# Attention and feed-forward layer on one core: x loaded once, split in rows, and turned by transposing transfers

## The chip, the cores and the metric

The kernel runs on 1 core of one Trainium2 chip. The metric is the device time of one execution, in microseconds (us); before the change it is 1840.24, the median of 3 runs (1839.78 to 1840.81). Engines are named as in the profile: PE is TensorE (matmuls, with PEld its weight loads), DVE VectorE, ACT ScalarE, POOL GpSimd, SP the engine whose queue issues the transfers.

## The reference

x has 8 sequences of 1024 tokens and 512 features. A layer of segmented attention with a memory is followed by a layer norm, then a feed-forward with quantized weights and a second layer norm:

```python
xs = x.reshape(b, n_seq, 128, d)                  # segments of 128 tokens
q, k, v = proj(Wq), proj(Wk), proj(Wv)            # 8 heads of 64
# for each segment, in order, with mem and z carried along:
sq = elu(q) + 1; att_mem = sq @ mem / (sq @ z)
sk = elu(k) + 1; mem = mem + sk^T v; z = z + sum(sk)
att = gate * att_mem + (1 - gate) * softmax(q k^T / 8) @ v
x = layernorm(x + att @ Wo)
h = relu(x @ quantize(W1)^T + b1)                 # 2048 wide
x = layernorm(x + h @ quantize(W2)^T + b2)
```

## The kernel before

The work is cut into 32 groups g, each of two sequences (t = 0, 1) at one segment of 128 tokens; two groups are alive at a time (LIVE = 2), so the memory of group g comes from group g - 2. Weights stay in SBUF. Operands of matmuls are float16 pairs: a high part and the rest, so that a product takes three matmuls (high by high, high by low, low by high). Each engine has its own hand-written order of work; in the loop `for g in range(2, NG + 2)` all engines work on the projections, scores and softmax of group g beside the feed-forward of g - 2 and g - 1. Semaphores alone tie the orders together.

PE in one turn of the loop (lines 577 to 616): `ffn_up(g-2, 1..4)`, `project_qk(g)` with `ffn_up(g-2, 5..7)` between, `project_out(g-1)`, `update_memory(g-1)`, `scores(g)`, `ffn_down(g-2, 0)`, `project_v(g)`, `ffn_down(g-2, 1, 0)`, `read_memory(g)` (line 378), the rest of `ffn_down`, `attend(g)` (lines 392 to 394), `ffn_up(g-1, 0)`. `read_memory(g, 0)` takes two PSUM banks that held scores of t = 1, so it waits for `p_lo(g, 1, 1)` (line 761). `ffn_up(g-1, 0)` waits for `attm`, the last piece of `read_scale(g, 1)` on DVE.

x before the change comes twice. `load_x` (line 1559) brings the rows of a group, needed for the residual, in one transfer. `load_blocks` (line 1572) brings the same values in 8 transfers of 64 KB, arranged so that DVE's 32 x 32 transpose (`turn_x`, line 696) completes the turning. Then:

- `group_max` (line 631) on DVE: largest |x| per partition, over `x_blocks`.
- `bounce_out` (line 1613) and `bounce_back` (line 1620) on SP: 128 values to DRAM and back, so that each partition has all of them.
- `all_max` (line 644) and `x_scale`, four small DVE instructions in a chain (the last is line 661).
- `xt_hi` (line 1170) on ACT and `xt_lo` (line 702) on DVE: the scaled, split, turned x in `xt`, 718 and 1096 ns each on average.
- `project_qk` and `project_v` on PE read `xt`.

Only group 0 has its x turned by PE. Three transposing transfers on SP are there already: `turn_p` (the softmax, line 1647), `turn_y` (line 1656) and `turn_att` (line 1639); the last two are of the size that x has, 128 x 1024 values of float16 to a t. `move_sk` (line 1632) issues 16 small transfers.

Ahead of the loop stands a start-up part in which PE also transposes the feed-forward weights (`turn_w`, line 280), ACT puts them (`put_w`, line 1296), and DVE rounds them (`round_w`, line 930). `turn_w(n)` waits for `put_w(n-2)`, so the two go in step. `sum_all(2)` on PE waits for a sum (line 919) that DVE forms behind `qk_split(1, "k", 0)`. `attend(0, 1)` waits for `turn_p(0, 1)`. `spread_bias_max` (line 514) waits for `bias_maximum` (line 940), which DVE does behind `att_scale(0, 1)`.

Of the kernel before, what the change touches and what calls it, by code (L numbers as in the profile page):

```python
# [32 lines left out]
    xblocks skblocks xturn xt_hi xt kproj qproj kq_exp klo qlo elu vproj v_hi v1 v  # L33
# [7 lines left out]
def build_program(nc, x, Wq, Wk, Wv, betas, Wo, W1, b1, W2, b2, out):  # L41
# [14 lines left out]
    with ctx:  # L56
# [31 lines left out]
        x_blocks = sb("x_blocks", [P, TG, D])  # L88
# [90 lines left out]
        def in_cols(blocks, t):  # L179
            return blocks[:, t].rearrange("p (k c) -> p k c", k=KT)  # L180

# [21 lines left out]
        def by_middle(g, t):  # L203
            return TG * (g - 1) + t + 1

# [38 lines left out]
        def _(pe):  # L244
# [38 lines left out]
            def project_qk(g, n, j):  # L283
# [6 lines left out]
                pe.wait_ge(sem["xt"], by_t(g, 1))  # L290
# [9 lines left out]
            def project_v(g, t):  # L300
# [5 lines left out]
                pe.wait_ge(sem["xt"], by_t(g, t))  # L306
# [312 lines left out]
        def _(dve):  # L619
            def group_max(g):  # L620
                if not 0 <= g < NG:
                    return
                if g == 0:
                    dve.wait_ge(s_x[0], 16)
                else:
                    dve.wait_ge(sem["xblocks"], 16 * 8 * g)
# [4 lines left out]
                dve.tensor_reduce(amax[:, g % 2:g % 2 + 1], x_blocks[:] if g else rows[:, 0], AX_XY, ALU.max,  # L631
# [60 lines left out]
            def turn_x(g, t):  # L692
                if not 0 <= g < NG:
                    return
                dve.wait_ge(sem["xblocks"], 16 * 8 * g)
                dve.transpose(x_blocks[:, t], x_blocks[:, t]).then_inc(sem["xturn"], 1)

            def xt_lo(g, t):
# [3 lines left out]
                dve.scalar_tensor_tensor(out=xt[:, t, KT:2 * KT], in0=in_cols(x_blocks, t) if g else x_bank(t), scalar=gcol(g, G_SCALE), in1=xt[:, t, 0:KT],  # L702
# [366 lines left out]
            turn_x(2, 0)  # L1069
            turn_x(2, 1)  # L1070
# [25 lines left out]
            for g in range(2, NG + 2):  # L1096
# [11 lines left out]
                h_split(g - 2, 7)  # L1108
                score_max(g, 0, 0)
# [4 lines left out]
                group_max(g + 1)  # L1114
# [6 lines left out]
                turn_x(g + 1, 0)  # L1121
                turn_x(g + 1, 1)
# [11 lines left out]
                all_max(g + 1)  # L1134
                x_scale(g + 1, 0)
# [3 lines left out]
                x_scale(g + 1, 1)  # L1139
                x_scale(g + 1, 2)  # L1140
                x_scale(g + 1, 3)
# [18 lines left out]
        def _(act):  # L1160
            def xt_hi(g, t):
                if not 0 <= g < NG:
                    return
                act.wait_ge(sem["xscale"], 4 * g + 4)
                if g:
                    act.wait_ge(sem["vproj"], by_t(g - 1, t))
                    act.wait_ge(sem["kproj"], 2 * g)
                    act.wait_ge(sem["qproj"], 2 * g)
                act.wait_ge(sem["xturn"], by_t(g, t))
                act.activation(xt[:, t, 0:KT], in_cols(x_blocks, t) if g else x_bank(t), ACT.Copy, scale=gcol(g, G_SCALE)).then_inc(sem["xt_hi"], 1)  # L1170
# [202 lines left out]
            for g in range(2, NG + 2):  # L1373
# [27 lines left out]
                v_split(g, 1)  # L1401
# [339 lines left out]
```

## Time and profile before

| | before |
|---|---|
| median of 3 runs | 1840.24 us |
| the profiled execution, its own time | 1839.69 us |
| its span, first to last instruction | 1837.9 us |
| PE busy | 1783.5 us (97%) |
| DVE busy | 1461.5 us (80%) |
| ACT busy | 997.0 us (54%) |
| POOL busy | 781.8 us (43%) |
| mean busy share of the DMA queue q1 | 45.6% of 16 engines |
| granted TensorE clock, mean | 0.99 |
| chain that ended last, share of PE | 95% |

A time in the trace is counted from the start of the span; 1.8 us of the execution lie around it. A busy engine is not necessarily what sets the end: the chain of work that ended last and the waits of an engine tell that. PE has 54.4 us in which it does nothing.

### The profile page before, as it was taken

Reading aid. Unit: us, or ns where it says so; the run is one execution under the profiler, and the core shown is the slowest. Engines: PE = TensorE matmul, PEld = TensorE weight load, DVE = VectorE, ACT = ScalarE, POOL = GpSimd, SP = SyncE. Lnnn points to the kernel's source line nnn. Section 1 sums busy time; section 2 is a strip of 40 time slices with the busy share of each in tenths; the row PEclk is TensorE's granted clock in tenths of the full one; section 3 lists DMA queues with packets and bytes.
Section 4 is the critical chain, followed back from the end, with each engine's and each line's share of the span. In section 5 each row is a group of like instructions: output and inputs, shape, how many; then the busy total and the mean of one; then the engine's idle time right before and its main releaser. Section 6 shows DMA issues by size and latency. Waiting matters only on the chain.

```text
span 1837.9 us, 42414 instructions
## 1 busy us (share of the span) xinstructions
PE 1783.5 (97%) x15935; PEld 1249.6 (68%) x15935; DVE 1461.5 (80%) x2807; ACT 997.0 (54%) x2422; POOL 781.8 (43%) x775
## 2 busy tenths in 40 slices
PE   4779999999999999999999999999999999999998
PEld 3556777766777766677766677766677776677765
DVE  7667788878888887888887888887878887888774
ACT  5765645555655555554655554655564555565542
POOL 0203444543444444354444354444344453444442
PEclk9889999999999999999999999999999999999999
DMA  8624435455445455435445534445543544443320
GB/s 281 150 38 78 74 73 90 59 88 87 73 76 93 61 84 91 83 67 90 71 72 93 86 66 85 77 66 94 87 71 78 86 63 89 89 74 73 60 47 24
DMA packets 555130, 150.87 MB, mean 82 GB/s; under 512 B 528544, under 2 KB 532528, under 8 KB 554416
## 3 DMA queue, kind: packets, MB, share of 16 engines
q1 hardware_dynamic: 554928, 148.16, 45.6%
q8 instruction: 129, 2.11, 0.5%
q14 instruction: 73, 0.60, 0.2%
HBM read 50.54 MB, written 16.80 MB: 37 GB/s over the span
## 4 chain that ended last, share of the span: by engine, by line
PE 95%; DVE 2%; ACT 2%; issue 1%; POOL 0%; DMA 0%; POOLq 0%; ACTq 0%; DVEq 0%
PE bank L464 12%; PE bank L465 12%; PE bank L448 12%; PE bank L449 12%; PE bank L294 6%; PE bank L295 6%; PE bank L296 6%; PE bank L378 3%; PE bank L426 3%; PE bank L428 3%; PE bank L427 3%; PE bank L308 3%; PE bank L310 3%; PE bank L309 3%; PE bank L413 2%; PE bank L327 1%
## 5 line engine op out<-in xcount | busy, mean ns | idle before, releaser
L448 PE MATMUL bank<-yt,w1t 128*128 128x256 f16 x2048 | 454.0, 273 | 0.6 <-ACT arena L1271 0.4
L449 PE MATMUL bank<-yt,w1t 128*128 128x256 f16 x2048 | 453.9, 273 | 0.0
L464 PE MATMUL bank<-w2t,arena 128*128 128x512 f16 x1024 | 388.7, 380 | 0.0
L465 PE MATMUL bank<-w2t,arena 128*128 128x512 f16 x1024 | 388.1, 379 | 0.0
L1271 ACT ACTIVATE arena<-bank,b_scaled,wscalars 128x256 f32<-128x256 f32 x512 | 261.2, 564 | 179.9 <-PE bank L449 108.6
L1215 ACT ACTIVATE bank<-bank,exp_bias,gscalars 128x128 f32<-128x128 f32 x512 | 220.5, 431 | 222.1 <-DVE exp_bias L752 222.1
L448 PEld LDWEIGHTS bank<-yt,w1t 128*128 128x128 f16 x2048 | 200.4, 98 | 24.2 <-ACT arena L1271 0.7
L449 PEld LDWEIGHTS bank<-yt,w1t 128*128 128x128 f16 x2048 | 200.4, 98 | 22.8
L875 DVE CAST arena<-arena 128x512 f16<-128x512 f32 x256 | 186.0, 727 | 7.5 <-ACT arena L1271 7.4
L1508 POOL TENSOR_TENSOR arena<-arena 128x512 f16<-128x512 f32 x128 | 155.2, 1213 | 68.6 <-DVE arena L875 68.6
L464 PEld LDWEIGHTS bank<-w2t,arena 128*128 128x128 f16 x1024 | 100.1, 98 | 118.6
L1430 POOL TENSOR_TENSOR att_mem<-att_mem,gate_in 128x512 f32<-128x512 f32 x60 | 76.1, 1268 | 239.2 <-DVE att_mem L791 239.2
L465 PEld LDWEIGHTS bank<-w2t,arena 128*128 128x128 f16 x1024 | 100.3, 98 | 113.4
L1170 ACT ACTIVATE xt<-x_blocks,gscalars 128x512 f16<-128x512 f32 x62 | 44.5, 718 | 220.7 <-DVE gscalars L661 220.6
L1452 POOL TENSOR_SCALAR var_eps<-mean_var 128x1 f32<-128x1 f32 x64 | 14.7, 229 | 326.5 <-DVE mean_var L856 326.5
L702 DVE SCALAR_TENSOR_TENSOR xt<-x_blocks,gscalars,xt 128x512 f16<-128x512 f32 x62 | 67.9, 1096 | 93.0 <-ACT xt L1170 93.0
L295 PE MATMUL bank<-xt,wk_hi 128*128 128x256 f16 x512 | 141.3, 276 | 0.0
L294 PE MATMUL bank<-xt,wk_hi 128*128 128x256 f16 x512 | 141.3, 276 | 0.0
L296 PE MATMUL bank<-xt,wk_lo 128*128 128x256 f16 x512 | 141.2, 276 | 0.0
L1473 POOL TENSOR_TENSOR y_rows<-rows,y_rows 128x512 f16<-128x512 f32 x60 | 68.1, 1156 | 171.6 <-ACT y_rows L1253 171.6
L294 PE MATMUL bank<-xt,wq_hi 128*128 128x256 f16 x512 | 139.5, 273 | 0.0
L296 PE MATMUL bank<-xt,wq_lo 128*128 128x256 f16 x512 | 139.5, 273 | 0.0
(180 smaller groups left out, 4358.5 us busy)
## 6 DMA issues: line engine op xcount, KB each, us to landing
rows<-in_L_attn_x SPq DMA_DIRECT2D x32, 512.0 KB, 3.9
out_rows<-rows SPq DMA_DIRECT2D x64, 256.0 KB, 2.4
x_blocks<-in_L_attn_x SPq DMA_DIRECT2D x248, 64.0 KB, 3.0
sk<-sk_t SPq DMA_DIRECT2D x480, 32.0 KB, 2.0
arena<-in_L_ffn_W SPq DMA_DIRECT2D x6, 1024.0 KB, 5.6
w2t<-in_L_ffn_W SPq DMA_DIRECT2D x2, 1024.0 KB, 13.1
w1t<-in_L_ffn_W SPq DMA_DIRECT2D x2, 1024.0 KB, 14.2
amax_row<-amax_dram SPq DMA_DIRECT2D x31, 64.0 KB, 3.1
```

The source lines that it names most:

```text
L294: pe.matmul(ps[:, :, c], w_hi[n][:, k, cols], xt[:, :, k], start=k == 0, stop=False)
L295: pe.matmul(ps[:, :, c], w_hi[n][:, k, cols], xt[:, :, KT + k], start=False, stop=False)
L296: ins = pe.matmul(ps[:, :, c], w_lo[n][:, k, cols], xt[:, :, k], start=False, stop=k == KT - 1)
L448: pe.matmul(ps[:, c], w1t[:, k, cols], yt[:, g % 2, :, k], start=k == 0, stop=False)
L449: ins = pe.matmul(ps[:, c], w1t[:, k, cols], yt[:, g % 2, :, KT + k], start=False, stop=k == KT - 1)
L464: pe.matmul(banks[own][:], h_hi[:, f, toks], w2t[:, f, :], start=f == 0, stop=False)
L465: ins = pe.matmul(banks[own][:], h_lo[:, f, toks], w2t[:, f, :], start=False, stop=f == FT - 1)
L875: dve.tensor_copy(hi, h32[:, n % NH32]).then_inc(sem["h_hi"], 1)
L1215: ins = act.activation(ps[:, c], ps[:, c], ACT.Exp, scale=gcol(g, G_EXP), bias=exp_bias[:, t, at:at + 1], accum_out=row_sum[:, t, h:h + 1])
L1271: ins = act.activation(h32[:, n % NH32, c * GT:(c + 1) * GT], ps[:, c], ACT.Relu, scale=w(H_SCALE_Y), bias=b1_scaled[:, f:f + 1])
L1430: pool.tensor_tensor(a, a, gate_in[:], ALU.mult).then_inc(sem["gated_in"], 1)
L1508: pool.tensor_tensor(lo, h32[:, n % NH32], hi, ALU.subtract).then_inc(sem["h_pool"], 1)
```

## The change

For all groups but 0, x comes once, in rows. ACT and DVE scale and split it in rows (into a new buffer `x_rows`, in the place of `x_blocks`), and two transposing transfers on SP put both halves into `xt`. The 8 block transfers and DVE's two transposes of a group go. The maximum is taken over the rows, and stands earlier in DVE's order: directly behind `h_split(g-2, 7)`, ahead of `score_max(g, 0, 0)`. `all_max`, `x_scale`, `xt_hi` and `xt_lo` stand earlier too, in front of or between `v_split(g, 1)`, `read_scale` and `residual(g-2, 0, 1)`. In the start-up, `xt_hi(1)` stands ahead of `put_w(0)`, and `project_qk(1, "k", 0)` behind `turn_w(11)` instead of ahead of `turn_w(8)`.

```diff
@@ buffers
-        x_blocks = sb("x_blocks", [P, TG, D])
+        x_rows = sb("x_rows", [P, TG, 2, D], F16)
+        def xt_there(g, t):
+            return (sem["xt"], t + 1) if g == 0 else (sem[f"xt{t}"], 16 * g)
@@ PE: project_qk and project_v
-                pe.wait_ge(sem["xt"], by_t(g, 1))
+                pe.wait_ge(*xt_there(g, 0))
+                pe.wait_ge(*xt_there(g, 1))
@@ PE, start-up
-            project_qk(1, "k", 0)
             for n in range(8, 12):
                 turn_w(n)
+            project_qk(1, "k", 0)
             sum_all(2)
@@ DVE: group_max
-                if g == 0:
-                    dve.wait_ge(s_x[0], 16)
-                else:
-                    dve.wait_ge(sem["xblocks"], 16 * 8 * g)
+                dve.wait_ge(s_x[g % NX], 16 * (g // NX + 1))
...
-                dve.tensor_reduce(amax[:, g % 2:g % 2 + 1], x_blocks[:] if g else rows[:, 0], AX_XY, ALU.max,
+                dve.tensor_reduce(amax[:, g % 2:g % 2 + 1], rows[:, g % NX], AX_XY, ALU.max,
@@ DVE: turn_x goes; xt_lo
+                if g:
+                    dve.scalar_tensor_tensor(out=x_rows[:, t, 1], in0=rows[:, g % NX, t], scalar=gcol(g, G_SCALE), in1=x_rows[:, t, 0],
+                                             op0=ALU.mult, op1=ALU.subtract).then_inc(sem["xt_lo"], 1)
+                    return
@@ DVE, start-up
             x_scale(1, 0)
-            turn_x(1, 0)
             x_scale(1, 1)
-            turn_x(1, 1)
             x_scale(1, 2)
             x_scale(1, 3)
             round_w(1)
+            xt_lo(1, 0)
+            xt_lo(1, 1)
             scale_sums(0, 0)
             scale_sums(0, 1)
             bias_columns()
-            xt_lo(1, 0)
             att_scale(0, 0)
-            xt_lo(1, 1)
@@ DVE, loop
                 h_split(g - 2, 7)
+                group_max(g + 1)
                 score_max(g, 0, 0)
...
                 p_lo(g, 0, 0)
-                group_max(g + 1)
                 score_max(g, 1, 0)
...
                 p_lo(g, 1, 0)
-                turn_x(g + 1, 0)
-                turn_x(g + 1, 1)
                 p_lo(g, 1, 1)
                 v_split(g, 0)
                 turn_sk(g)
                 invert_sums(g, 0)
+                all_max(g + 1)
+                x_scale(g + 1, 0)
                 v_split(g, 1)
+                x_scale(g + 1, 1)
+                x_scale(g + 1, 2)
                 read_scale(g, 0)
+                x_scale(g + 1, 3)
                 read_scale(g, 1)
+                xt_lo(g + 1, 0)
+                xt_lo(g + 1, 1)
                 residual(g - 2, 0, 1)
...
-                all_max(g + 1)
-                x_scale(g + 1, 0)
...
-                xt_lo(g + 1, 0)
                 att_scale(g, 1)
-                xt_lo(g + 1, 1)
@@ ACT: xt_hi
+                    if g > 1:
+                        act.wait_ge(sem[f"xt{t}"], 16 * (g - 1))
+                    act.wait_ge(s_x[g % NX], 16 * (g // NX + 1))
+                    ins = act.activation(x_rows[:, t, 0], rows[:, g % NX, t], ACT.Copy, scale=gcol(g, G_SCALE))
@@ ACT, start-up
             w_sum(2, 0)
-            for n in range(0, 4):
+            xt_hi(1, 0)
+            xt_hi(1, 1)
+            for n in range(0, 8):
                 put_w(n)
-            xt_hi(1, 0)
-            for n in range(4, 8):
-                put_w(n)
-            xt_hi(1, 1)
             w_sum(2, 1)
-            qk_split(1, "k", 0)
             for n in range(8, 12):
                 put_w(n)
+            qk_split(1, "k", 0)
@@ ACT, loop: xt_hi(g+1, 0) and (g+1, 1) stand directly behind v_split(g, 1)
@@ SP: load_blocks goes; new
+            def turn_x(g, t):
+                if not 0 <= g < NG:
+                    return
+                sp.wait_ge(sem["xt_lo"], TG * (g - 1) + t + 1)
+                sp.wait_ge(sem["kproj"], 2 * g)
+                sp.wait_ge(sem["qproj"], 2 * g)
+                sp.wait_ge(sem["vproj"], by_t(g - 1, t))
+                sp.dma_start_transpose(xt[:, t], x_rows[:, t].rearrange("p c n -> p (c n)")).then_inc(sem[f"xt{t}"], 16)
@@ SP, start-up (in the place of load_blocks(1) stands load_x(1); turn_x(1, 0..1) ahead of move_sk(0), turn_x(2, 0..1) ahead of move_sk(1))
@@ SP, loop
             for g in range(2, NG + 2):
-                load_blocks(g + 1)
                 bounce_out(g + 1)
                 turn_p(g, 0)
                 turn_y(g - 1, 0)
                 turn_y(g - 1, 1)
+                bounce_back(g + 1)
                 turn_p(g, 1)
-                bounce_back(g + 1)
+                turn_x(g + 1, 0)
+                turn_x(g + 1, 1)
                 move_sk(g)
```

## Rows read from the trace of the kernel before

**Rows 1.** Busy time by stretch: one period; us, PE, PEld, DVE, ACT, POOL, PEclk, DMA.

```profile
957.80:1012.50 54.70, 54.70 (x499) 38.31 (x497) 45.22 (x87) 29.85 (x74) 24.31 (x24) 1.00 0.49 80
```

**Rows 2.** Waits of PE from 130 us on, the longest in total.

```profile
PE bank L392 <- issue: 0.6, 1, 0.6
```

**Rows 3.** Timeline of ACT in the start-up: start, length, instruction, idle before.

```profile
60.08 1.29 ACT L1296 ACTIVATE w1t<-bank,unround 128x512 f16<-128x512 f32 x2
...
63.44 0.71 ACT L1170 ACTIVATE xt<-x_blocks,gscalars 128x512 f16<-128x512 f32 x1
```

**Rows 4.** Timeline of DVE in the start-up.

```profile
61.09 0.70 DVE L696 STREAM_TRANSPOSE x_blocks<-x_blocks 128x512 f32<-128x512 f32 x1
...
62.51 0.16 DVE L661 RECIPROCAL gscalars<-gscalars 128x1 f32<-128x1 f32 x1
...
79.14 0.15 DVE L919 TENSOR_REDUCE wscalars<-wscalars 128x1 f32<-128x4 f32 x1
```

**Rows 5.** Timeline of PE in the start-up.

```profile
67.92 0.19 PE L392 MATMUL bank<-v_hi,pt 128*128 128x64 f16 x1 [0.69 <-issue]
...
71.28 0.38 PE L514 MATMUL bank<-wscalars,ones_all 1*128 1x1 f32 x2 [2.50 <-DVE wscalars L940]
...
75.89 1.04 PE L280 MATMUL bank<-ident,arena 128*128 128x128 f32 x8
78.53 1.24 PE L280 MATMUL bank<-ident,arena 128*128 128x128 f32 x8 [1.61 <-ACT w1t L1296]
```

**Rows 6.** Busy time by stretch (columns as in rows 1), behind PE's 2.50 us of idleness.

```profile
72.10:75.50 3.40, 3.40 (x18) 2.34 (x17) 3.09 (x15) 0.00 (x0) 0.29 (x1) 0.50 0.31 48
```

**Rows 7.** Timeline of SP's queue in the start-up: turn_p(0, 1).

```profile
58.30 5.99 SPq L1647 DMA_TRANSPOSE pt<-p_rows  x1
```

**Rows 8.** Timeline of DVE, POOL and PEld within one period.

```profile
926.21 0.68 DVE L747 TENSOR_REDUCE row_max<-bank 128x4 f32<-128x512 f32 x1
926.95 1.15 POOL L1508 TENSOR_TENSOR arena<-arena 128x512 f16<-128x512 f32 x1
927.03 1.10 DVE L752 TENSOR_SCALAR exp_bias<-row_max,gscalars 128x4 f32<-128x4 f32 x1
...
928.86 0.23 DVE L752 TENSOR_SCALAR exp_bias<-row_max,gscalars 128x4 f32<-128x4 f32 x1
...
931.42 1.21 DVE L631 TENSOR_REDUCE amax<-x_blocks 128x1 f32<-128x1024 f32 x1
...
939.19 0.69 DVE L761 SCALAR_TENSOR_TENSOR p_rows<-bank,p_rows 128x512 f16<-128x512 f32 x1 [0.54 <-ACT p_rows L1226]
...
940.52 0.64 PEld L378 LDWEIGHTS bank<-mem,sq_t 64*128 64x128 f32 x10 [0.42 <-issue]
```

**Rows 9.** Timeline of SP's queue within the same period.

```profile
919.12 0.39 SPq L1559 DMA_DIRECT2D rows<-in_L_attn_x  x1
...
942.56 3.00 SPq L1647 DMA_TRANSPOSE pt<-p_rows  x1
...
946.28 11.23 SPq L1632 DMA_DIRECT2D sk<-sk_t  x16
```

**Rows 10.** Timeline of DVE and PE, rest of the period and the next one's start.

```profile
909.55 1.18 DVE L722 SCALAR_TENSOR_TENSOR sk_t<-exp_tmp,relu_tmp 128x512 f32<-128x512 f32 x1
...
942.02 0.16 DVE L768 RECIPROCAL inv_sum<-row_sum 128x8 f32<-128x8 f32 x1
...
949.04 0.27 PE L448 MATMUL bank<-yt,w1t 128*128 128x256 f16 x1
...
957.78 0.27 PE L294 MATMUL bank<-xt,wk_hi 128*128 128x256 f16 x1
```

**Rows 11.** The page, issues: KB each, median us from issue to landing.

```profile
rows<-in_L_attn_x SPq DMA_DIRECT2D x32, 512.0 KB, 3.9
...
amax_row<-amax_dram SPq DMA_DIRECT2D x31, 64.0 KB, 3.1
...
at<-att_dot SPq DMA_TRANSPOSE x60, 3.1
```

More of the change, by code:

```diff
@@ L32 @@
     amax amax_row amax_cell amax_all xscale sc0 sc1 sc2 sc3
-    xblocks skblocks xturn xt_hi xt kproj qproj kq_exp klo qlo elu vproj v_hi v1 v
+    skblocks xturn xt_hi xt_lo xt xt0 xt1 kproj qproj kq_exp klo qlo elu vproj v_hi v1 v
     score rowmax exp_bias pexp pt_hi pt_lo pt0 pt1 skturn
@@ L690, in scalars @@
                     dve.tensor_scalar(gcol(g, G_WO), gcol(g, G_AINV), w(INV_W["o"]), None, ALU.mult).then_inc(sem["sc3"], 1)
[L692 to L696, printed above, removed]
             def xt_lo(g, t):
@@ L701, in xt_lo @@
                 dve.wait_ge(sem["xt_hi"], by_t(g, t))
[L702 removed]
+                if g:
+                    dve.scalar_tensor_tensor(out=x_rows[:, t, 1], in0=rows[:, g % NX, t], scalar=gcol(g, G_SCALE), in1=x_rows[:, t, 0],
+                                             op0=ALU.mult, op1=ALU.subtract).then_inc(sem["xt_lo"], 1)
+                    return
+                dve.scalar_tensor_tensor(out=xt[:, t, KT:2 * KT], in0=x_bank(t), scalar=gcol(g, G_SCALE), in1=xt[:, t, 0:KT],
                                          op0=ALU.mult, op1=ALU.subtract).then_inc(sem["xt"], 1)
@@ L1165, in xt_hi @@
                 if g:
[L1166 to L1170, printed above, removed]
+                    if g > 1:
+                        act.wait_ge(sem[f"xt{t}"], 16 * (g - 1))
+                    act.wait_ge(s_x[g % NX], 16 * (g // NX + 1))
+                    ins = act.activation(x_rows[:, t, 0], rows[:, g % NX, t], ACT.Copy, scale=gcol(g, G_SCALE))
+                else:
+                    act.wait_ge(sem["xturn"], t + 1)
+                    ins = act.activation(xt[:, t, 0:KT], x_bank(t), ACT.Copy, scale=gcol(g, G_SCALE))
+                ins.then_inc(sem["xt_hi"], 1)
             def qk_split(g, n, j):
@@ L1401, in _ @@
                 v_split(g, 1)
+                xt_hi(g + 1, 0)
+                xt_hi(g + 1, 1)
                 if g - 1 in EDGES:
@@ L1405, in _ @@
                     yt_hi(g - 1, 1)
-                xt_hi(g + 1, 0)
                 h_relu(g - 1, 0)
                 h_relu(g - 1, 1)
-                xt_hi(g + 1, 1)
                 h_relu(g - 1, 2)
@@ L1559, in load_x @@
                 sp.dma_start(rows[:, g % NX], src).then_inc(s_x[g % NX], 16)
-            def load_blocks(g):
+            def turn_x(g, t):
                 if not 0 <= g < NG:
                     return
-                b0, seg, _ = place(g)
-                if g > 1:
-                    sp.wait_ge(sem["xt"], by_t(g - 1, 1))
-                for t in range(TG):
-                    src = x[b0 + t, seg * P:(seg + 1) * P, :].rearrange("(b j) (k a i) -> a j k b i", j=32, a=4, i=32)
-                    for a in range(4):
-                        dst = x_blocks[32 * a:32 * a + 32, t].rearrange("p (k b i) -> p k b i", k=KT, b=4)
-                        sp.dma_start(dst, src[a]).then_inc(sem["xblocks"], 16)
+                sp.wait_ge(sem["xt_lo"], TG * (g - 1) + t + 1)
[3 more added lines that the diff above has]
+                sp.dma_start_transpose(xt[:, t], x_rows[:, t].rearrange("p c n -> p (c n)")).then_inc(sem[f"xt{t}"], 16)
             def load_w(n):
@@ L1677, in _ @@
             sp.dma_start(b2_all[:], b2.partition_broadcast(P)).then_inc(sem["b2_load"], 16)
-            load_blocks(1)
+            load_x(1)
             load_ffn_w(2, 0)
@@ L1686, in _ @@
             turn_p(0, 1)
+            turn_x(1, 0)
+            turn_x(1, 1)
             move_sk(0)
-            load_x(1)
             load_x(2)
             load_ffn_w(2, 2)
-            load_blocks(2)
             load_ffn_w(2, 3)
+            load_x(3)
             bounce_out(2)
@@ L1696, in _ @@
             bounce_back(2)
+            turn_x(2, 0)
+            turn_x(2, 1)
             move_sk(1)
@@ L1699, in _ @@
             turn_att(1, 1)
-            load_x(3)
             for g in range(2, NG + 2):
-                load_blocks(g + 1)
                 bounce_out(g + 1)
```

9 lines of the change are left out of this document (1 added, 8 removed).

## The prediction

> **What bounds the kernel now.** I read the windows first, one for each turn of the loop. A turn lasts 54.70 us and PE is busy in all of it, at the full clock [rows 1]. The waits of PE from 130 us on say the same: the longest is 0.6 us, once [rows 2]. So in the loop nothing that is taken off DVE, SP or the transfers can shorten the time: DVE is busy 45 of 54.7 us, yet PE never stands for it. A gain can come only from PE's 54 idle us, nearly all in the start-up, and a loss from a piece that now reaches PE late. Both need timelines, of the start-up and of one turn. There the reader is to look at the start of a PE instruction and at the end of what releases it.
>
> **The loop, part by part.** *Removed:* 8 block transfers, two DVE transposes of 0.70 us [rows 4]. Worth nothing: PE covers them. If that cover went, each transpose would be worth its 0.70.
>
> *The maximum, moved ahead of score_max(g, 0, 0).* It reads rows that load_x issues at 919.12 and that land 3.9 us later, 923.0 [rows 9, 11]; DVE comes to it at 926.21 [rows 8]. So it does not wait, with 3.2 us to spare. Its 1.21 us now stand in front of the scores' maximum. But exp_bias is held behind a POOL subtraction until 928.1, and takes 1.10 us instead of 0.23 [rows 8]. With the maximum in front it would start at 926.21 + 1.13 + 0.82 = 928.16, when POOL is through, and end at 928.39 instead of 928.13. So ACT's exponentials, and p_lo at the end of their chain, come 0.3 us later. p_lo(g, 1, 1) ends at 939.88 and read_memory begins at 940.52: 0.6 us to spare [rows 8]. I take no wait; the bounds of the shift are 0 and 1.21.
>
> *The way round through DRAM.* Before, the values went out when the maximum ended, at 932.6 [rows 8]; now at 927.4. bounce_back takes the place of turn_p(g, 1), which was issued at 942.56 [rows 9], and lands 3.1 us later [rows 11]: 945.7 at the latest. DVE reaches all_max at about 942.4, behind invert_sums [rows 10] and the 0.3 us. Wait: 0 to 3.3 us. SP's queue was slow there with the small transfer to DRAM ahead of the transposes; that is now 5 us earlier, so I take 0. What stands behind: v_split(g, 1), x_scale, both read_scale, some 4 us, and then ffn_up(g-1, 0) may start; it starts at 949.04 [rows 10]. Without the wait DVE is there at 946.5, 2.5 us ahead.
>
> *Split and turn.* xt_hi follows at about 945.4 and takes 0.71 [rows 3] twice; xt_lo follows read_scale(g, 1), 1.1 us each, so it ends between 948 and 949. A transposing transfer of this size lands 3.1 us after its issue [rows 11], and the second is issued over a us behind the first: xt is there by 951 to 953. project_qk begins at 957.78 [rows 10]. About 5 us to spare.
>
> By the Trainium skill (SBUF — State Buffer, "Who interferes with whom") a DVE instruction with two inputs in SBUF is shut out for the whole of a POOL instruction that reads SBUF. That speaks against xt_lo here, beside POOL's gating: it would put some 1.5 us on each xt_lo; the 5 us still cover it, and the sum is the same by both.
>
> *What is moved behind it.* residual(g-2, 0, 1) comes about 3 us later, and with it POOL's second variance, add_bias and the gating. Their reader on ACT, at_hi(g, 1), stands behind h_relu of the next turn, over a us later: covered. move_sk (16 issues, 11.2 us from 946.28 [rows 9]) now waits for the two turns of x, until about 950 to 951, and ends, with its last landing, near 963; the next writing of sk_t, which waits for it, is at 909.55 + 54.7 = 964.2 [rows 1, 10]. Covered by about 1 us, and behind that DVE's own room before the next scores. turn_p(g, 1) has one short issue put in front, but a queue less crowded: the 0.6 us of attend(g, 1) [rows 2], which I ascribe to a late turned softmax, should go. **Loop: -0.6 us.**
>
> **The start-up**, where PE is the bound only in part.
> 1. xt_hi(1) now stands ahead of put_w(0). The scale is ready at 62.67 [rows 4], less some 0.9 for the two transposes between: 61.8. ACT then does two xt_hi of 0.71 [rows 3]. put_w(0) starts near 63.0 instead of 60.08 [rows 3]: +2.9. Until then ACT stands idle.
> 2. PE's turn_w(2) to (7) go in step with put_w: +2.9. attend(0, 1) waited 0.69 us before, for its turned softmax [rows 5]; this is absorbed: 70.1 instead of 67.92, +2.2.
> 3. Between attend(0, 1) and spread_bias_max lay 3.4 us, and PE idle for 2.50 of them [rows 5]. In it DVE waited for ACT's second xt_hi and did xt_lo(1, 1) and a rounding, which now come before. So the distance shrinks: I take +0.7 for spread_bias_max (bounds 0 and +2.2), which ends at 72.4.
> 4. turn_w(8) to (11) come next: 1.04 + 1.24 us [rows 5] and a short wait. project_qk(1, k, 0) starts at 74.9 instead of 71.66 [rows 5]: **+3.2**. The turned x is issued once turn_p(0, 1) is off SP, at 64.3 [rows 7], and so lands near 70: it does not set this.
> 5. project_qk(1, k, 0) took 4.2 us, to 75.89, 3.4 of them at the half clock, 1.2 GHz, behind PE's 2.50 idle us [rows 5, 6]. Now it comes behind transposes with about 1 us of idleness; I take the full clock: **-1.7** (bounds -1.7 and 0). It ends at 77.4.
> 6. sum_all(2) needs the sum at 79.14 [rows 4], which stands on DVE behind qk_split(1, k, 0): 3.4 us after the projection's end. Before, turn_w(8) to (11) filled that time, until 79.77 [rows 5]. Now nothing does, and PE idles 3.7 us. No term of its own (the sum now comes at 77.4 + 3.7 = 81.1, 1.5 later than before), but the clock: behind 2.50 idle us a stretch of 3.4 us ran at the half clock [rows 6], and this idleness is longer. Half of 3.40: **+1.7** (bounds 0 and 1.7).
> Behind it every step waits for the one before on PE, ACT or DVE until the loop, so nothing is given back. **Start-up: 3.2 - 1.7 + 1.7 = +3.2**, with bounds +1.5 and +4.9. The fewer transfers there are worth nothing: the weights' loads wait for splits on DVE.
>
> By the Trainium skill (TensorE: Matmul & The Clock Gate, "What's actually happening") idleness throttles PE and work releases it. It says nothing other than rows 6 about the second hole, but it makes the terms of steps 5 and 6 differ between executions, as the moment of the switch is not tied to the kernel.
>
> **The sum.** The profiled execution took 1839.69 us (span 1837.9 and 1.8 around it), 0.55 below the median. 1839.69 + 3.2 - 0.6 = 1842.3; as a median, 1842.9 (+0.14%).
>
> **The rivals.**
> *A: the way back from DRAM is late in every turn.* If bounce_back is issued only at 942.56, as turn_p was, and lands at 945.7, DVE stands 3.3 us in front of all_max, and the 4.1 us of work behind it end at 949.8, against 949.04 [rows 9 to 11]. PE stands 0.75 us in each of 30 turns: +22, 1865. It decides once the values land later than about 944.9. For it: that turn's queue. Against: the queue should be freer. Chance 0.12.
> *B: the maximum delays the softmax in full.* If p_lo(g, 1, 1) shifts by 1.21 instead of 0.3, it passes the margin of 0.64 by 0.57 [rows 8]: 30 x 0.57 = +17, 1860. It decides at a shift of 0.64. Against: the arithmetic on exp_bias. Chance 0.10.
> *C: the start-up gives the delay back*, say because PE's later holes absorb it: 1839.5 to 1840.5. Against: those holes follow the scores, which are themselves late. Chance 0.10.
> *D: faster.* No row has 3.7 us for it: only the 0.6, and a start-up in which the half clock is escaped and step 1 is nearly hidden, 1836. Chance 0.06.
> The forecast has 0.62.
>
> **Range and chances.** About 0.2%, 3.7 us, is what a measurement of this kernel can tell from no change: 1836.6 to 1843.9. The forecast's own bounds are +1.5 - 0.6 and +4.9 - 0.6, so 1841.1 to 1844.5; its upper end, above 1843.9, gets 0.12. Slower: 0.12 + 0.12 + 0.10 = 0.34. Same: 0.50 + 0.10 = 0.60. Faster: 0.06. The range runs from 1839 to 1860: it takes in C and most of B, and leaves out A's far end and D, under 2 in 10. The likeliest case's own is 1841.1 to 1844.5.
>
> **What would show it.** Right: turns of 54.7 us with PE busy throughout; project_qk(1, k, 0) near 75, then a hole of 3.7 us before sum_all(2); DVE busy some 40 us less (62 transposes at 0.70); the 0.6 us gone. Wrong: a wait of PE in every turn ahead of ffn_up (A) or read_memory (B), or of project_qk on a transfer; or a loop that starts no later than before (C).

## The result, and the profile after

The changed kernel takes 1846.97 us, the median of 6 runs (1845.01 to 1847.83), beside 1840.18 of the kernel before (1839.64 to 1840.81, 6 runs): a ratio of 1.0036, 95% interval 1.0026 to 1.0045. It is slower by 6.8 us. The profiled execution took 1846.83 us, with a span of 1845.0. One run of e12 (7124 us) and two of the kernel before in the batches of the experiments (3613 and 6618 us) fell into a slow state and are left out of all ranges and ratios below.

The page, busy time and the shares of the chain that ended last:

```profile
PE 1784.8 (97%) x15935; PEld 1250.0 (68%) x15935; DVE 1411.5 (77%) x2745; ACT 1003.4 (54%) x2422; POOL 763.7 (41%) x775
...
PE 68%; DVE 12%; ACT 6%; POOL 4%; issue 4%; SPq 3%; DMA 3%; ACTq 0%; DVEq 0%; POOLq 0%
```

DVE is busy 50 us less than before, and PE as long as before; yet the chain, 95% PE before, now goes through DVE, ACT, POOL, SP's queue and a transfer. PE's idle time has grown.

Busy time by stretch, for three turns of the loop in the changed kernel (columns as in [rows 1]):

```profile
467.70:522.40 54.70, 54.70 (x498) 38.31 (x497) 41.95 (x81) 30.16 (x74) 22.87 (x24) 1.00 0.45 79
522.40:577.60 55.20, 54.81 (x499) 38.41 (x498) 43.09 (x85) 30.05 (x74) 24.01 (x25) 1.00 0.46 79
...
907.50:963.80 56.30, 55.02 (x499) 38.47 (x498) 44.64 (x88) 29.94 (x74) 25.02 (x27) 1.00 0.43 78
```

The first is like the turn of [rows 1]: 54.70 us, PE busy in all of it. The other two are longer. Measured from the start of one project_qk(g, k, 0) to the next, the turns g = 9, 10 and 13 to 18 take 54.86 to 56.22 us, the rest 54.70. That makes +4.8 us. Before, one turn was longer by 0.8, which is gone: the loop stands at **+4.0**. Group 2's projection starts at 139.5 us instead of 136.5: the start-up stands at **+3.0**.

The waits of PE from 130 us on, against [rows 2]:

```profile
PE bank L379 <- DVE p_rows L757: 3.3, 7, 0.7
PE bank L328 <- DVE rows L841: 0.8, 2, 0.6
```

read_memory (L379) waits for p_lo (L757), the end of the softmax. And DVE's own waits from 130 us on:

```profile
DVE gscalars L642 <- DMA amax_row<-amax_dram: 27.5, 23, 2.0
...
DVE sk_t L718 <- DMA sk<-sk_t: 3.1, 3, 2.5
```

In 23 turns DVE stands in front of all_max (L642) because the maximum is not back from DRAM. Here is that place in a turn that stays at 54.70 (it starts at 303.6), SP's queue first, then DVE, with the next maximum (L629) and what comes before it:

```profile
340.00 0.53 SPq L1607 DMA_DIRECT2D amax_row<-amax_dram  x1
...
343.06 0.29 DVE L642 TENSOR_REDUCE gscalars<-amax_row 128x1 f32<-128x128 f32 x1
...
360.48 1.37 DVE L859 TENSOR_SCALAR rows<-rows,mean_var,rstd 128x512 f32<-128x512 f32 x1 [2.00 <-POOL rstd L1450]
...
376.94 0.75 DVE L841 SCALAR_TENSOR_TENSOR rows<-bank,gscalars,rows 128x512 f32<-128x512 f32 x1 [0.59 <-PE bank L429]
...
379.53 0.75 DVE L841 SCALAR_TENSOR_TENSOR rows<-bank,gscalars,rows 128x512 f32<-128x512 f32 x1 [0.89 <-PE bank L429]
...
381.49 1.22 DVE L629 TENSOR_REDUCE amax<-rows 128x1 f32<-128x1024 f32 x1
```

And in the turn that starts at 522.4, with what PE does at the end:

```profile
559.53 0.54 SPq L1607 DMA_DIRECT2D amax_row<-amax_dram  x1
...
564.41 0.29 DVE L642 TENSOR_REDUCE gscalars<-amax_row 128x1 f32<-128x128 f32 x1 [1.89 <-DMA amax_row<-amax_dram]
...
581.82 1.37 DVE L859 TENSOR_SCALAR rows<-rows,mean_var,rstd 128x512 f32<-128x512 f32 x1 [2.00 <-POOL rstd L1450]
...
597.61 0.75 DVE L841 SCALAR_TENSOR_TENSOR rows<-bank,gscalars,rows 128x512 f32<-128x512 f32 x1
...
599.24 0.75 DVE L841 SCALAR_TENSOR_TENSOR rows<-bank,gscalars,rows 128x512 f32<-128x512 f32 x1
...
601.54 1.21 DVE L629 TENSOR_REDUCE amax<-rows 128x1 f32<-128x1024 f32 x1
...
614.79 0.69 DVE L757 SCALAR_TENSOR_TENSOR p_rows<-bank,p_rows 128x512 f16<-128x512 f32 x1 [1.76 <-ACT p_rows L1219]
...
615.58 1.67 PE L379 MATMUL bank<-mem,sq_t 64*128 64x65 f32 x26 [0.49 <-DVE p_rows L757]
```

Read the square brackets. In both turns DVE waits 2.00 us for POOL's variance (L1450): that wait is no slack, since POOL got its input from DVE and moves with it. What is slack is the 0.59 and 0.89 us in which DVE waits for PE's project_out (L429): 1.48 us in all. In the late turn (522.4) all_max starts 2.55 us later within the turn (42.01 against 39.46), those two gaps are gone, and the next maximum starts 1.25 us later (79.14 against 77.89). Behind it come the scores, ACT's exponentials and p_lo, and PE stands. The way back decides once all_max starts behind about 39.5 + 1.5 = 41 us of a turn. In this kernel it starts anywhere from 39.4 to 42.9, and the trace divides cleanly: the eight turns that follow an all_max at 41.08 us or later are the eight late ones, and no turn that follows one at 40.84 or earlier is late.

The start-up, PE (against [rows 5]), SP's queue and DVE:

```profile
64.01 1.97 PE L280 MATMUL bank<-ident,w2t 128*128 128x128 f32 x8 [4.86 <-ACT w1t L1289]
...
72.31 0.38 PE L515 MATMUL bank<-wscalars,ones_all 1*128 1x1 f32 x2 [1.04 <-DVE wscalars L936]
...
81.20 0.38 PE L507 MATMUL bank<-wscalars,ones_all 128*128 128x1 f32 x2 [3.29 <-DVE wscalars L915]
...
66.88 10.56 SPq L1619 DMA_DIRECT2D sk<-sk_t  x16
...
80.40 0.68 DVE L718 SCALAR_TENSOR_TENSOR sk_t<-exp_tmp,relu_tmp 128x512 f32<-128x512 f32 x1
```

PE stands 4.86 us for put_w(0), 1.04 for the bias's maximum, and 3.29 in front of sum_all(2), the hole of the prediction's step 6. The last two rows come up again: move_sk(0), now issued from 66.88 us on, behind the turned x, and DVE's writing of the tile that it reads, without a wait here.

### The profile page after: what moved, and what is told of

Its sections match the earlier page's. It is cut to its first block, busy times and chain, and to the rows that moved or that the text cites. A ratio compares the mean times of both kernels' runs of the same rounds, so it can differ in the third digit from the quotient of the medians.

```text
span 1845.0 us, 42230 instructions
## 1 busy us (share of the span) xinstructions
PE 1784.8 (97%) x15935; PEld 1250.0 (68%) x15935; DVE 1411.5 (77%) x2745; ACT 1003.4 (54%) x2422; POOL 763.7 (41%) x775
## 4 chain that ended last, share of the span: by engine, by line
PE 68%; DVE 12%; ACT 6%; POOL 4%; issue 4%; SPq 3%; DMA 3%; ACTq 0%; DVEq 0%; POOLq 0%
PE bank L449 9%; PE bank L450 9%; PE bank L465 9%; PE bank L466 8%; PE bank L295 4%; PE bank L296 4%; PE bank L297 4%; ACT bank L1208 3%; PE bank L379 2%; PE bank L427 2%; PE bank L429 2%; PE bank L428 2%; DMA amax_row<-amax_dram 2%; PE bank L309 2%; PE bank L311 2%
## 5 line engine op out<-in xcount | busy, mean ns | idle before, releaser
L1421 POOL TENSOR_TENSOR att_mem<-att_mem,gate_in 128x512 f32<-128x512 f32 x60 | 81.5, 1359 | 291.3 <-DVE att_mem L787 291.3
L871 DVE CAST arena<-arena 128x512 f16<-128x512 f32 x256 | 193.0, 754 | 8.5 <-ACT arena L1264 8.4
L757 DVE SCALAR_TENSOR_TENSOR p_rows<-bank,p_rows 128x512 f16<-128x512 f32 x128 | 88.5, 692 | 140.5 <-ACT p_rows L1219 140.5
L1499 POOL TENSOR_TENSOR arena<-arena 128x512 f16<-128x512 f32 x128 | 148.6, 1161 | 74.7 <-DVE arena L871 74.7
L859 DVE TENSOR_SCALAR rows<-rows,mean_var,rstd 128x512 f32<-128x512 f32 x128 | 104.6, 838 | 60.3 <-POOL rstd L1450 60.3
L874 DVE TENSOR_TENSOR arena<-arena 128x512 f16<-128x512 f32 x128 | 145.4, 1136 | 4.4
L1180 ACT ACTIVATE exp_tmp<-bank,gscalars 128x512 f32<-128x512 f32 x128 | 87.8, 686 | 101.4 <-DVE sk_t L718 98.4
```

Source lines behind the costliest of these rows:

```text
L871: dve.tensor_copy(hi, h32[:, n % NH32]).then_inc(sem["h_hi"], 1)
L874: dve.tensor_tensor(lo, h32[:, n % NH32], hi, ALU.subtract).then_inc(sem["h_dve"], 1)
L1499: pool.tensor_tensor(lo, h32[:, n % NH32], hi, ALU.subtract).then_inc(sem["h_pool"], 1)
```

## The experiments

Three theories were open for the loop: the values come back late (the one I held by now), the maximum ahead of the scores uses up the softmax's margin (the prediction's rival B), the transfers of sk are late of themselves. For the start-up: my six steps, against rival C. All edits are to the changed kernel. In this table "late" counts turns over 54.75 us among g = 2 to 29, and "group 2" is when its projection starts; both are of the profiled execution, the rest of all runs.

| run | median (range), us | ratio to before, 95% | late | group 2 |
|---|---|---|---|---|
| changed | 1846.97 (1845.0 to 1847.8) | 1.0036 (1.0026 to 1.0045) | 8 | 139.5 |
| e1 | 1842.97 (1841.6 to 1843.9) | 1.0016 (1.0007 to 1.0025) | 0 | 141.2 |
| e2 | 1913.25 (1910.4 to 1913.7) | 1.0397 (1.0382 to 1.0412) | 28 | 139.2 |
| e3 | 1847.68 (1846.1 to 1848.8) | 1.0043 (1.0029 to 1.0058) | 9 | 140.4 |
| e4 | 1884.37 (1884.1 to 1884.9) | 1.0244 (1.0229 to 1.0258) | 27 | 139.5 |
| e5 | 1842.61 (1841.6 to 1843.6) | 1.0014 (1.0005 to 1.0022) | 0 | 141.2 |
| e6 | 1845.79 (1841.7 to 1849.6) | 1.0027 (1.0018 to 1.0036) | 8 | 138.1 |
| e7 | 1846.48 (1845.2 to 1849.6) | 1.0036 (1.0024 to 1.0049) | 7 | 142.5 |
| e8 | 1843.58 (1843.2 to 1844.1) | 1.0018 (1.0010 to 1.0027) | 0 | 141.6 |
| e9 | 1841.05 (1839.5 to 1843.4) | 1.0007 (0.9998 to 1.0016) | 0 | 140.9 |
| e10 | 1839.07 (1837.5 to 1841.3) | 0.9994 (0.9985 to 1.0003) | 0 | 135.6 |
| e11 | 1836.31 (1835.4 to 1837.4) | 0.9980 (0.9971 to 0.9988) | 0 | 134.0 |
| e12 | 1842.57 (1841.2 to 1844.6) | 1.0016 (1.0006 to 1.0025) | 0 | 139.4 |

### The loop

**e1, the way back issued earlier.**

```diff
                 turn_p(g, 0)
+                bounce_back(g + 1)
                 turn_y(g - 1, 0)
                 turn_y(g - 1, 1)
-                bounce_back(g + 1)
                 turn_p(g, 1)
```

> Edit: bounce_back(g + 1) is issued directly behind turn_p(g, 0), ahead of turn_y(g - 1, 0) and (g - 1, 1). Changed kernel: 1847.0, its loop +4.0 over the kernel before, in 8 turns of 54.86 to 56.22 us among 24 of 54.70. Theory (the values come back late: issued at 36.4 us of a turn, landing at 39.4 to 42.9, and a turn whose all_max starts behind about 40.8 makes the next one late): the values now land near 36, DVE no longer waits for them before all_max, which starts near 39.2 in every turn; all turns of the loop 54.70, no wait of PE at read_memory, the start-up's +3.0 stays: 1842 to 1843.5. Rival (the maximum in front of the scores uses up the softmax's margin): the margin of 0.37 us ahead of read_memory is the same, late turns stay: 1846 to 1848. Rival (the transfers of sk behind the turned x are late of themselves): all_max is early but sk still lands behind 62 us in some turns, PE waits stay in part: 1844 to 1847.

Measured: the values land at 36.6 to 38.1 us of a turn instead of 39.4 to 42.9, all_max starts at 39.3 us in nearly every turn without a wait, and every turn of the loop takes 54.70 us. What PE still waits for from 130 us on:

```profile
PE bank L449 <- ACT arena L1264: 0.4, 1, 0.4
PE bank L427 <- DVE at L825: 0.2, 1, 0.2
PE bank L328 <- DVE rows L841: 0.2, 1, 0.2
PE bank L449 <- ACT w2t L1289: 0.2, 1, 0.2
```

From group 2 to the end of the span this kernel takes 1842.0 - 141.2 = 1700.8 us; the changed one took 1705.5 and the one before 1701.4. The loop's +4.0 is gone, and the -0.6 that the prediction gave it is there. The theory stands; the maximum and the transfers of sk kept their places in the order, so neither place alone makes turns late.

**e2, the way back issued later.**

```diff
-                bounce_back(g + 1)
                 turn_p(g, 1)
+                bounce_back(g + 1)
```

> Edit: bounce_back(g + 1) is issued behind turn_p(g, 1) instead of ahead of it. Theory (the way back sets the late turns): it is issued a little over 1 us later and lands behind the turned softmax, at 42.5 to 44 us of a turn; all_max starts behind 42.5 in every turn, the next group_max late in nearly every one, turns of 55.2 to 56.5 on average: 1860 to 1895. Rival (maximum in front, or transfers of sk, set them): as the changed kernel, 1846 to 1850.

Measured: 1913.25, beyond the range of the theory, and far from the rivals. Two waits share it, and DVE's stands behind both:

```profile
PE bank L449 <- DVE att_mem L787: 34.2, 29, 1.9
PE bank L379 <- DVE p_rows L757: 21.2, 29, 1.0
...
DVE gscalars L642 <- DMA amax_row<-amax_dram: 105.4, 29, 4.3
```

The first row is the one that the expectation left out: it is exactly rival A's wait, PE in front of ffn_up(g-1, 0) for read_scale. With all_max at 43.2 to 45.1 us it comes on top of the wait at read_memory. The response is steep: values that land 3.6 us later on average than in the changed kernel (44.2 us of the turn for 40.5) cost 66 us.

**e4, the maximum where it was.**

```diff
-                group_max(g + 1)
                 score_max(g, 0, 0)
...
                 p_lo(g, 0, 0)
+                group_max(g + 1)
```

> Edit: group_max(g + 1) goes back behind p_lo(g, 0, 0), where the kernel before had it. Rival B (the maximum ahead of the scores takes the margin before read_memory): the softmax is 0.26 us earlier again, the margin back at 0.64, the late turns go: 1842 to 1844. Theory (late way back): the values go out some 5 us later, near 29.5 us of a turn, reach DRAM at 36.5 to 38, and come back at 41.5 to 44; all_max is late in every turn and the next turn's maximum and scores with it: more late turns than now, 1850 to 1890.

Measured: 1884.37. exp_bias is 0.26 us earlier again (25.05 for 25.31 us of the turn, before any turn is late), and it gains nothing, as the values now leave for DRAM at 29.6 to 31.4 us of a turn, come back at 41.8 to 45.6, and 27 turns are late; PE stands 14.0 us at ffn_up(g-1, 0) and 13.8 at read_memory. By itself this does not rule B out, since the edit gives the margin back and delays the values in one. e1 does: there the maximum stands ahead of the scores as in the changed kernel, exp_bias ends at the same 25.31 us, and no turn is late. What e4 does show is that with bounce_back where it is, the early maximum is needed.

**e3, half of sk's transfers ahead of the turned x.**

```diff
+                move_sk(g, (0, 1))
                 turn_x(g + 1, 0)
                 turn_x(g + 1, 1)
-                move_sk(g)
+                move_sk(g, (2, 3))
```

> Edit: half of move_sk's 16 transfers go ahead of turn_x(g + 1, 0), the other half behind turn_x(g + 1, 1). The values come back from DRAM as late as in the changed kernel. If the late turns come from sk_t being overwritten too late (DVE waits for the last transfer of sk before it turns the next sums): the last landing falls from 60-63.6 us to about 58, DVE's wait for sk goes, turns 54.70 for nearly all: 1843 to 1844.5. If they come from POOL and DVE working on the second half of the feed-forward later and at the same time (residual late, its variance, the gating, h_split): no change, 1846 to 1848. A price of its own: turn_x may be issued up to 5.6 us later than now when at_hi's inputs are in time; 5 us were free ahead of project_qk, so a wait of PE on the turned x would show this.

This was for the reading that the chain of waits suggests. In the changed kernel, for the late turn shown above, it goes like this (start, length, what):

```profile
559.53 4.85 DMA amax_row<-amax_dram
...
570.50 2.17 SPq L1559
...
582.57 3.41 DMA sk<-sk_t
586.00 0.86 DVE sk_t L718
...
614.79 0.70 DVE p_rows L757
615.58 1.45 PE bank L379 x22
```

By that, the way back delays DVE, DVE the turned x, that the 16 transfers of sk, and their last landing the next writing of sk_t. Measured: the last landing comes at 55.5 to 58.3 us of a turn instead of 59.4 to 63.7, and 9 turns are late, those of the changed kernel and one more, by much the same amounts (the turn g = 9 takes 55.13 for 55.15). The transfer was a second path of nearly the same length, not the cause. The chain names one releaser where two came almost together.

**e5, the residual ahead of all_max.** The transfers keep their places; only DVE's order changes.

```diff
                 invert_sums(g, 0)
+                residual(g - 2, 0, 1)
                 all_max(g + 1)
...
                 xt_lo(g + 1, 1)
-                residual(g - 2, 0, 1)
```

> Edit: residual(g - 2, 0, 1), with its statistics, goes ahead of all_max(g + 1) on DVE again, as in the kernel before; the transfers stay as in the changed kernel, so the values still land at 39.4 to 42.9 us of a turn. Theory (DVE has only some 1.5 us of idleness of its own between all_max and the next maximum, its waits for POOL's variance and for ACT being part of the chain; a way back that lands behind 40.8 uses it up): the residual's 1.6 us now fill the wait for the values instead of standing behind it, so values may land up to about 42.4 before anything is late; nearly all turns 54.70, no or one wait of PE at read_memory: 1842 to 1844.5. Rival (the transfers set the late turns in another way, by the turned x or by sk, which stay as late): 1846 to 1848. A price of its own would be a wait of DVE for the second half of ffn_down, of which the trace of the changed kernel shows none.

Measured: 1842.61, no late turn, as good as e1, although the values land at 39.3 to 41.1 us, all_max starts at 40.8 to 41.2, and the last of sk's transfers lands at 60.9 to 63.3. DVE now waits for the values 0.6 us in all (27.5 in the changed kernel), since the residual's 1.6 us fill that time, and for POOL's variance 25.4 instead of 60.3 us, since POOL got its input earlier. It even waits for sk, and PE does not notice:

```profile
DVE sk_t L718 <- DMA sk<-sk_t: 45.3, 29, 3.3
```

With e1 this shows what was lost: DVE's time between the way back and the next maximum. It can be given back from either side. (e5 gives it back in two ways at once, by the filled wait and by POOL's earlier start; it does not tell their shares.)

### The start-up

**e6, the projection ahead of turn_w(8) to (11) again** (PE's order, then ACT's).

```diff
+            project_qk(1, "k", 0)
             for n in range(8, 12):
                 turn_w(n)
-            project_qk(1, "k", 0)
...
+            qk_split(1, "k", 0)
             for n in range(8, 12):
                 put_w(n)
-            qk_split(1, "k", 0)
```

> Edit, start-up alone: project_qk(1, k, 0) stands ahead of turn_w(8) to turn_w(11) again, on ACT qk_split(1, k, 0) ahead of put_w(8); the loop is that of the changed kernel. My steps 4 and 6 (the projection behind the transposes leaves a hole before sum_all(2)): the projection starts near 72.7 us instead of 75.1 and ends at 75.2 (full clock) or 76.9 (half clock); sum_all(2) starts at 79 to 80.5 instead of 81.2, the hole of 3.3 us is gone, the loop begins 0.7 to 2 us earlier: 1845 to 1846.3. Rival (the sum's moment is set by DVE's work elsewhere, or the clock takes it back): as the changed kernel, 1846.5 to 1847.5.

**e7, and on ACT xt_hi(1) between put_w(3) and put_w(4).**

```diff
+            for n in range(0, 4):
+                put_w(n)
             xt_hi(1, 0)
             xt_hi(1, 1)
-            for n in range(0, 8):
+            for n in range(4, 8):
                 put_w(n)
```

> Edit, start-up alone: as the one before, and on ACT xt_hi(1, 0) and (1, 1) stand behind put_w(3) instead of ahead of put_w(0). My step 1 (xt_hi ahead of put_w(0) holds ACT idle until the scale is there, +2.9): put_w(0) starts near 60.1 again, attend(0, 1) near 68, the turned x lands near 70, project_qk(1, k, 0) starts near 71, and the loop begins at 136 to 137 instead of 139.5: 1843 to 1844.5, the loop's +4.0 staying. Rival C (PE's later holes set the loop's beginning anyway): 1846 to 1847.5.

**e8, the edits of e7 and e1 together.**

> Edit: the two edits of the start-up together with bounce_back(g + 1) directly behind turn_p(g, 0). By the theory both losses are gone and the loop keeps its gain of 0.6 to 0.8 us over the kernel before: 1838 to 1840, the kernel before being 1840. Rival (the start-up is longer for another reason, such as the clock's half-speed stretches behind project_v): 1841 to 1843.

Measured: e6 1845.79, within what was expected, but its runs lie 8 us apart, which drowns the start-up. I put that down to late turns that differ from run to run; only one run of each kernel has a trace, so it is not shown, but in the kernels without late turns the runs lie 0.9 to 3.9 us apart. From here on the loop of e1 was kept. e7 and e8 are misses: 1846.48 and 1843.58, not a bit better than without the edits, though put_w(0) starts at 61.1 us in e8 for 63.29 and the projection at 71.0 for 75.1. The waits of e8 in the start-up tell why, DVE first, then PE:

```profile
81.05 0.69 DVE L718 SCALAR_TENSOR_TENSOR sk_t<-exp_tmp,relu_tmp 128x512 f32<-128x512 f32 x1 [4.70 <-DMA sk<-sk_t]
...
81.86 0.58 PE L507 MATMUL bank<-wscalars,ones_all 128*128 128x1 f32 x2 [4.37 <-DVE wscalars L915]
```

The sum for sum_all(2) stands on DVE behind the writing of group 1's sk_t, and that waits for move_sk(0), whose 16 transfers SP now issues behind the turned x of group 1, from 69.08 to 79.6. Before, they went from 64.3 on. The delay that the prediction put down to the projection alone has a second floor: in the changed kernel the last of the 16 lands at 78.8 us, 1.6 us before DVE writes the tile at 80.40, and undoing the first only lays it bare. It is a relative of rival C that I had not thought of: with the first delay undone, a later wait sets the start of the loop.

**e9, e6 with the early way back; e10, e9 with group 0's turned sums in a tile of their own** (room in yt that is not yet used), so that nothing waits for move_sk(0); **e11, e8 with that tile; e12, e1 with that tile.**

```diff
+        sk_t0 = yt[:, 1].rearrange("p t k n -> p (t k n)").bitcast(F32).rearrange("p (t c n) -> p t c n", t=TG, c=NPAIR)
...
-                elif 0 < g <= NG - LIVE:
+                elif 1 < g <= NG - LIVE:
                     dve.wait_ge(sem["skblocks"], MOVED * g)
...
-two_pairs(sq_t if n == "q" else sk_t, j)
+two_pairs(sq_t if n == "q" else sk_t if g else sk_t0, j)
```

> Edit: project_qk(1, k, 0) ahead of turn_w(8) as in the run e6, with bounce_back(g + 1) directly behind turn_p(g, 0), so that the loop adds nothing that varies. My steps 4 and 6: the projection behind the transposes costs the start-up its hole of 3.3 us and, in some executions, a half-clock stretch of 1.7 us behind it; undone, group 2's projection starts near 138.1 us instead of 141.2, the clock stays full from 80 to 108 us: 1840 to 1841. Rival (the place of the projection is not what the start-up loses by): as the run with the early way back, 1842.5 to 1843.5.

> Edit: as e9, and group 0's turned sums are written to a tile of their own (room that yt has free then), so DVE no longer waits for move_sk(0)'s last transfer before it writes group 1's (1.7 us in e6). Theory (move_sk(0), now behind turn_x(1, 1) on SP, is a second bound of the start-up): the sum is there about 1.7 us earlier, at 78 us, and PE waits for ACT's put_w(11) alone, sum_all(2) near 79.6 instead of 80.1: 1839 to 1840.5, 0.5 to 1.4 less than e9. Rival (no bound): as e9.

> Edit: as e8 (both edits of the start-up, early way back), and group 0's turned sums in a tile of their own. In e8 DVE waited 4.7 us for move_sk(0)'s last transfer, PE 4.4 us behind it, and then ran 80 to 87 us at the half clock. Theory (that transfer took over as the bound of the start-up once the rest was undone): the sum is there near 77.2 us instead of 81.7, sum_all(2) near 77.5, full clock behind it, group 2's projection at 134.5 to 137 instead of 141.6: 1836.5 to 1840. Rival (the loads of the feed-forward's weights, which SP issues behind move_sk(0) at 80.3, or another wait take over): PE stands in front of a later turn_w or of the feed-forward, 1840 to 1842.5.

> Edit: group 0's turned sums in a tile of their own, with the early way back, and the start-up otherwise that of the changed kernel. Theory (the transfer of sk bounds the start-up only once the projection is early: in the changed kernel DVE writes group 1's sums at 80.4 us, behind k_lo, without a wait for it): nothing, as the run with the early way back: 1842 to 1843.8. Rival (the tile itself is what made e11 fast, the order on ACT and PE mattering little): 1837 to 1841.

Measured: e9 1841.05, 1.9 less than e1, at the edge of the expected 1840 to 1841; its ratio to the kernel before can't be told from 1. Its runs fall in two clumps, six at 1839.5 to 1841.1 and five at 1842.1 to 1843.4, and the profiled one (1843.3) is of the upper, so the 1.9 is a rough figure. e10 1839.07, 2.0 less than e9, somewhat more than expected. e11 1836.31, 7.3 less than e8, faster than the kernel before by 3.8 us, ratio 0.9980 (0.9971 to 0.9988). e12 1842.57, within 0.4 of e1: the tile alone brings nothing, because the projection is then the later of the two. In e11, DVE and PE at the place where e8 stood:

```profile
75.88 0.68 DVE L719 SCALAR_TENSOR_TENSOR sk_t<-exp_tmp,relu_tmp 128x512 f32<-128x512 f32 x1
...
76.94 0.28 PE L508 MATMUL bank<-wscalars,ones_all 128*128 128x1 f32 x2
```

sum_all(2) starts at 76.94 us, without a wait, for 81.20 in the changed kernel and 79.61 before. This version beats both kernels.

**The clock behind the hole.** Three kernels, busy time by stretch at the place (columns as in [rows 1]): the changed kernel, e1, e11.

```profile
80.00:84.00 4.00, 2.80 (x26) 2.58 (x27) 2.72 (x7) 0.60 (x1) 0.00 (x0) 1.00 0.83 333
```

```profile
82.00:87.30 5.30, 5.30 (x27) 3.93 (x27) 2.20 (x4) 0.60 (x1) 0.00 (x0) 0.51 0.36 142
```

```profile
76.00:104.00 28.00, 25.40 (x258) 20.51 (x258) 17.40 (x30) 17.53 (x36) 1.51 (x4) 1.00 0.36 121
```

In e1 sum_all(2) comes behind a hole of 3.3 us, as in the changed kernel, and the 5.3 us shown run at 1.2 GHz; in the changed kernel's profiled execution that place runs at 2.4 GHz. Then both come to PE's idleness ahead of project_v, the changed kernel first, e1 below it:

```profile
118.90 0.61 PE L309 MATMUL bank<-wv_hi,xt 128*128 128x512 f16 x1 [6.18 <-DVE p_rows L757]
```

```profile
121.86 0.61 PE L309 MATMUL bank<-wv_hi,xt 128*128 128x512 f16 x1 [6.18 <-DVE p_rows L757]
```

The two run sum_all(2) within 0.2 us of each other (81.20 and 81.37), and project_v 3.0 us apart: 2.8 for the clock. Behind project_v's start the half clock lasts until 124.2 us in the changed kernel and until 124.7 in e1, so the changed kernel has more of project_v in it and e1 gets 1.2 us back. Group 2's projection starts 1.7 us later in e1.

Where the hole is gone (e10, e11) the clock is full. Behind a hole of 3.3 us it stayed full in the changed kernel and in e4, and fell in e1, e2, e3, e5 and e12; behind the holes of 4.3 and 4.4 us in e7 and e8 it fell too. e6 and e9 have the same order in the start-up, with holes of 1.61 us and then 1.42 (e6) or 1.23 (e9): the clock stays full in e6's profile and falls in e9's. The length of the hole does not tell by itself which way it goes.

## Why the prediction was right or wrong

The time lay in the range, 1839 to 1860. But the forecast was 1842.9, no change that can be measured, with a range of its own to 1844.5; the result is 1846.97, 2.5 beyond that, and slower. It takes part of two rivals. That the time lies in the range is owed to the range's width, which had been made to take in rival B, and not to the mechanism: the part on the loop has the wrong sign.

**The start-up, +3.2: right in size, and nearly in every step.** Step 1: put_w(0) at 63.0 predicted, 63.29 measured. Step 2: attend(0, 1) at 70.1, measured 70.4. Step 3: spread_bias_max to end at 72.4, measured to start at 72.31 and end at 72.69. Step 4: the projection at 74.9, measured 75.1. Step 5: the full clock, as taken (1.00 from 69.6 to 110 us). Step 6: a hole of 3.7 us and the sum at 81.1; measured 3.29 and 81.00. Its half clock, +1.7 in the sum, did not come in the profiled execution of the changed kernel nor in e4's. With the same order of the start-up it came in e2, e3 and e12 for 3.4 us, which delays project_v by 1.5 to 1.7 us, and in e1 and e5 for 6.8 us, which delays it by 2.7 to 2.8. At sum_all(2) the delay was thus 1.6 us (81.20 for 79.61 before). The other 1.4 came behind it: the stretch at the half clock around PE's 6.2 us of idleness ahead of project_v, which both kernels have, lasted from 110.6 to 124.2 us for 109.6 to 119.9 before, with more of project_v in it. So the sum came to +3.0 with one term off and another in its stead; that part is luck. As a median the start-up costs some +3 to +4: e1 has the loop of the prediction, and stands 3.2 over the kernel before, 3.8 with the loop's 0.6 added. What the steps missed is the second floor: "the turned x is issued once turn_p(0, 1) is off SP" counted the turned x, and not what SP issues behind it, move_sk(0). It cost nothing in the changed kernel, 4.7 us of DVE's time once the rest was undone.

**The loop, -0.6: wrong, +4.0.** The 0.6 itself was there (0.8 in the trace), and e1 shows it with nothing on top. Two steps failed together.

The first is the size of the wait at all_max: "Wait: 0 to 3.3 us ... I take 0". The values went out at 24.4 us of the turn and reached DRAM 6.5 to 8.3 us after their issue, so that was not what held them. bounce_back is issued at 36.4 to 38.3, behind the two turned y (e1, which puts it ahead of them, issues it at 32.6 to 34.8); that is up to 3.1 us earlier than the 39.5 us (942.56) that I gave as the latest. It then lands 2.9 to 4.9 us later, median 3.5, where I took 3.1. DVE is there at 39.3 to 39.4, as predicted (942.4 - 903.1). The wait is 0 to 2.0 us, 27.5 in all. The argument "the queue should be freer" did not settle it. The row to go by was one that I did not list: the same wait of DVE in the kernel before, from 130 us on.

```profile
DVE gscalars L644 <- DMA amax_row<-amax_dram: 13.1, 12, 2.9
```

There the values were called back later still (945.7 us, 42.6 of the turn) and all_max stood behind the residual; the transfer was late for it in 12 turns already, and PE never felt it. I moved all_max forward past the residual in the sum and kept no room for the transfer.

The second is "What is moved behind it ... covered". I followed POOL's reader on ACT and the transfers of sk, and left out DVE itself. DVE waits for POOL's variance, so a later residual makes the whole rest of DVE's turn later, and against that DVE has 1.48 us, not the 9.5 us that 45 busy of 54.7 seem to leave. POOL's gating also moved beside h_split: its subtraction (L874, two inputs in SBUF) took 0.69 us alone and 1.64 beside POOL's large instructions, 1136 ns on average for 928 before; with four of them to a turn that is 0.8 us of DVE's time in each, in e1 too. By the Trainium skill (SBUF — State Buffer, "Who interferes with whom") such an instruction contends with a POOL instruction that reads SBUF, and the trace agrees. For xt_lo, where the prediction weighed the rule, it had nothing to do: 29 of the 62 start in the last 0.1 us of POOL's gating, the rest stand alone, and all 62 took 741 to 752 ns. The kernel before had nearly all of its xt_lo beside POOL's gating, at 1096 ns on average.

**Rival A** had the right cause at the wrong place. In the changed kernel PE does not wait ahead of ffn_up(g-1, 0); that takes all_max behind about 43 us, as in e2. **Rival B** had the right place (read_memory behind p_lo) and the wrong cause: the maximum moves the softmax by 0.26 us, 0.3 predicted, and leaves 0.37 of the 0.64. That thin margin is why a DVE 1.25 us late reaches PE. **Rival C**, that a later wait sets the start of the loop anyway, did not hold for the changed kernel; in e7 and e8 such a wait took over.

DVE's busy time was to fall by some 40 us and fell by 50. What was said of project_qk on a transfer held: the turned x lands at 47.4 to 52.9 us of a turn, and PE never waits for it there.

## What to carry to other kernels

A wait of an engine for another that it feeds itself is no slack: count only waits for engines that do not depend on it, here 1.5 of 9.5 idle us, before you say that a delay is covered. When something new is put on an ordered queue, list everything issued behind it as well, in the start-up as in the loop, and who waits for the last of that. And where undoing a cause brings nothing, look for a second bound just under the first before you drop the theory; where runs scatter because one stage is at its limit, repair that stage first, and measure the rest on the quiet version.

## What the runs showed that was not expected

- The 512 bytes of the maximum take 6.5 to 8.3 us (median 7.0) from issue to landing in DRAM, and 2.9 to 4.9 us on the way back, for a value that DVE has to have in the same turn. e4, which sends them some 5 us later, pays for that directly.
- The late turns come in a row (13 to 18). In them the maximum goes out at 24.8 to 26.2 us of the turn for 24.4, and bounce_back is issued at 36.8 to 38.3; but turns that are not late issue it at up to 37.7 too, so that the delay is carried from turn to turn fits the trace and is not shown. The changed kernel's runs differ by 2.8 us, e6's by 8, the kernel before by 1.2.
- The half clock came behind a hole of PE of 1.2 us in one kernel and not behind 3.3 us in another. Between the changed kernel and e1 it moves the start of the loop by 1.5 us. It may be a part of the scatter of the runs and of e9's two clumps; with one trace for each kernel that is not shown.
